# A Mamba-style mixer on TensorE: the z projection of a feature tile issued directly behind its x projection, ahead of the turning of x

## The reference, cut to what matters

```python
proj = input_states @ in_proj_w.T
gate, hBC, dt = jnp.split(proj, [INTER, INTER + CONV_DIM], axis=-1)
x = conv_general_dilated(hBC..., conv_w)              # 4 taps, each feature for itself
hBC = silu(x + conv_b)
hs, Bmat, Cmat = jnp.split(hBC, ...)
xh = hs * dt                                          # and D_res = D * hs
Y_diag = einsum('bclsh,bcshp->bclhp', (C B^T) * exp(segsum(A dt)), xh)
states = einsum('bclhn,bhcl,bclhp->bchpn', Bc, decay_states, xh)   # then carried over chunks
Y_off = einsum('bclhn,bchpn,bhcl->bclhp', Cc, states, exp(A_cum))
y = Y_diag + Y_off + D_res
yg = y * silu(gate)                                   # gate is the "z" of the kernel
out = (norm_w * yg * rsqrt(mean(yg * yg) + EPS)) @ out_proj_w.T
```

## Time and profile before

| what | us |
|---|---|
| median of 3 runs | 2565.89 |
| lowest and highest of them | 2563.54, 2573.93 |
| the profiled execution's own time | 2581.05 |
| its span, first to last instruction | 2579.2 |
| mean granted TensorE clock, share of full | 0.886 |

### The profile page before, as it was taken

The page is one execution under the profiler, slowest core; times in us unless marked ns, Lnnn a source line. Parts: engine busy times, 40 slices in busy tenths (PEclk is TensorE's granted clock), DMA queues, the critical chain, the costliest instruction groups (busy, mean ns, idle before and its releaser), DMA issues.

```text
span 2579.2 us, 45536 instructions
## 1 busy us (share of the span) xinstructions
PE 2068.7 (80%) x12038; PEld 1584.6 (61%) x12043; DVE 1610.5 (62%) x3542; ACT 1416.2 (55%) x3825; POOL 1000.2 (39%) x816
## 2 busy tenths in 40 slices
PE   5896969789459345999999999999999954278883
PEld 4555555455347234888878887888788842156662
DVE  5545555454424476888888888888888863043334
ACT  1443525344224145888878887888788840035542
POOL 0301103030256210444444444444444416737774
PEclk8896978889679676999999999999999976589997
DMA  3451917030446601444434443444344352248878
GB/s 125 159 173 51 290 51 234 1 118 0 181 95 107 166 17 64 137 146 146 147 129 146 146 147 129 146 146 147 130 147 146 114 163 89 103 78 133 133 127 189
DMA packets 193524, 328.61 MB, mean 127 GB/s; under 512 B 19712, under 2 KB 141184, under 8 KB 191104
## 3 DMA queue, kind: packets, MB, share of 16 engines
q1 hardware_dynamic: 162208, 287.54, 35.3%
q0 software_dynamic: 31200, 39.73, 9.8%
HBM read 227.54 MB, written 99.66 MB: 127 GB/s over the span
## 4 chain that ended last, share of the span: by engine, by line
PE 63%; issue 11%; DVE 8%; DMA 4%; POOL 4%; ACT 3%; another core or an unknown queue 3%; PEldq 1%; DVEq 1%; ACTq 1%; SPq 1%; PEld 0%; POOLq 0%
PE bank L1717 14%; PE bank L1771 8%; PE bank L755 6%; PE bank L1745 5%; POOL expert_sums L1107 4%; PE bank L728 4%; PE bank L1764 3%; PE bank L1757 3%; PE bank L744 3%; PE bank L1731 3%; DMA expert_sums<-experts_yo,experts_xt 2%; PE bank L989 2%; PE bank L1740 2%; PE bank L730 2%
## 5 line engine op out<-in xcount | busy, mean ns | idle before, releaser
L1717 PE MATMUL bank<-h_hi,wi 128*128 128x512 f32 x1024 | 404.1, 436 | 0.8 <-ACTq L144 0.8
L1879 DVE SCALAR_TENSOR_TENSOR cv<-bank,cw,cv 128x511 f32<-128x511 f32 (+2 forms) x384 | 287.5, 749 | 84.9 <-ACT cv L1812 51.8
L1107 POOL DMA_INDIRECT expert_sums<-experts_yo,experts_xt x174 | 270.4, 1554 | 144.9 <-ACT experts_yo L1074 117.9
L1806 ACT ACTIVATE l_mat<-l_mat,cum_tok 128x128 f32<-128x128 f32 x1024 | 315.7, 429 | 0.0
L1931 POOL TENSOR_TENSOR xdec<-xdt,dec_tok 128x384 f32<-128x384 f32 x128 | 108.1, 844 | 467.2 <-DVE xdt L1869 467.2
L1946 POOL TENSOR_TENSOR yg<-yd,sgt 128x512 f32<-128x512 f32 x128 | 228.2, 1783 | 76.2 <-DVE yd L1886 76.2
L1198 DVE SCALAR_TENSOR_TENSOR experts_sg<-experts_th,bank 128x96 f32<-128x96 f32 (+2 forms) x190 | 53.9, 284 | 312.8 <-ACT experts_th L1067 187.8
L1771 PE MATMUL bank<-wo,yg 128*128 128x256 f32 x1024 | 242.4, 380 | 0.3 <-POOL yg L1946 0.3
L1717 PEld LDWEIGHTS bank<-h_hi,wi 128*128 128x128 f32 x1024 | 196.1, 191 | 62.7 <-issue 24.2
L579 DVE TENSOR_REDUCE nmax<-bank 128x1 f32<-128x512 f32 (+3 forms) x256 | 114.4, 487 | 177.7 <-PE bank L730 177.7
L657 ACT ACTIVATE work<-bank,nmax 128x512 f32<-128x512 f32 (+3 forms) x256 | 132.8, 525 | 150.1 <-DVE nmax L579 149.9
(11 more groups left out here) (292 smaller groups left out, 4711.0 us busy)
## 6 DMA issues: line engine op xcount, KB each, us to landing
wi<-in_weights_split SPq DMA_DIRECT2D x128, 512.0 KB, 3.5
l_mat<-running_sums SPq DMA_DIRECT2D x128, 512.0 KB, 4.6
experts_xt<-sorted_rows SPq DMA_DIRECT2D x174, 129.0 KB
wo<-out_weights_normed SPq DMA_DIRECT2D x128, 128.0 KB, 2.1
sorted_rows<-blank SPq DMA_DIRECT2D x1, 16383.0 KB, 61.5
expert_sums<-blank SPq DMA_DIRECT2D x6, 2176.0 KB, 17.7
experts_got<-expert_sums SPq DMA_DIRECT2D x24, 512.0 KB, 8.5
w_raw<-in_wi SPq DMA_DIRECT2D x32, 256.0 KB, 3.0
```

Source lines behind the costliest of these rows:

```text
L1107: e.indirect_dma_start(sums[layer][q % SPREAD], bass.IndirectOffsetOnAxis(xt[:, q % LOADED, D + 1:D + 2].bitcast(U32), 0), yo[:, q % YIELD ...
L1717: mm = e.matmul(dst[:, :], l, r[:, k, tok], start=(n == 0), stop=(n == 3 * KD - 1))
L1806: last = e.activation(part, part, ACT.Relu, bias=cum_tok[:, c, hh, bass.ds(w.g, 1)], scale=-1.0)
L1879: e.scalar_tensor_tensor(out=cv[:, w.two, n:SEQ], in0=PSX[w.two][:, 0:SEQ - n], scalar=cw[:, bass.ds(w.f, 1), TAPS - 1 - n], in1=cv[:, w.t ...
```

## The change

On PE, the block that issues the z projection of `tiles[0]` moves up: it now stands directly behind the x projection of the same tile, ahead of T of `tiles[1]` and of the y products of `tiles[3]`. Its wait (`s_sg` of the tile before) and its signal (`s_z`) move with it. No instruction is added or removed, and the lists of DVE, ACT, POOL and SP stay as they are.

```diff
             e.wait_ge(s_wi[w.four], w.loaded_i)
             e.wait_ge(s_tap, done(w.g - 2, 3))
             project(w, PSX[w.two], D, s_x)
+        w = tiles[0]
+        if w.live:
+            e.wait_ge(s_sg, done(w.g - 1))
+            project(w, PSZ, 0, s_z)
         w = tiles[1]
         if w.live:
             e.wait_ge(s_xc, done(w.g))
@@
             mm.then_inc(s_y, 1)
-        w = tiles[0]
-        if w.live:
-            e.wait_ge(s_sg, done(w.g - 1))
-            project(w, PSZ, 0, s_z)
         w = tiles[1]
         if w.live:
             e.wait_ge(s_xdec, done(w.g))
```

## The result

The changed kernel takes 2620.16 us (median of 4 runs, 2614.51 to 2625.42) against 2567.18 of before (4 runs beside it): a ratio of 1.020, 95% interval 1.017 to 1.023, or 44 to 59 us slower. Forecast was 2611, range 2593 to 2631.

A forecast was written before the change was run, and what follows sets the result against it. A ring of ACT and DVE was taken to hold the step at 8.06 us; loop steps +40, fixed-index steps +5.8, four others +2.5, boundaries -2.3, start +1, drain -0.5 gave +46.5, rounded +45: 2611 us, range 2593 to 2631.

The forecast's parts named there:

- The bound before: Loop step before the change: ACT and DVE hold it at 8.06 us; PE alone could do 7.83.
- rival (c): Faster: PE is the bound and z covers its 0.23 wait for `st` in 100 steps; 2541 us, chance 0.05.
- the ring through POOL: T, `xdt`, `xdec`, SS, off-diagonal y, output, x, z, back to T: forecast at 8.46 us a step.
- The chain T, `xdt`, `xdec`, SS: From T over DVE and POOL to SS: 2.52, plus 0.1 for SS behind a wait, 2.62 us; PE idle about 0.6.
- The ring: T to next T in the changed loop: 2.62 + 5.84 = 8.46 us, 0.40 more a step.
- Steps at the turn of the loop: No term in the sum; loop steps expected all alike, 0.95 to `xdec` used only for the range's high end.
- Steps with fixed indices: 12 short steps with fixed indices: 8.31 us each, +0.48 each, +5.8 us in all.
- Boundaries and start: Three group boundaries 0.75 us earlier each, -2.3; second step of the stream waits for `sgt`, +1; drain at the end -0.5.
- The sum: Whole stream: all terms together +46.5 us, rounded to +45, for a median of 2611 us.
- (a): PE's clock falls because of the pauses: 2650 us if every fourth step, 2770 if every step; chance 0.04.
- (b): No measurable difference: T to SS within 2.22 us, step stays 8.06, only boundaries gain; 2564 us, chance 0.06.
- (d): z on PE waits for `sgt` in every step, and T with it; 2636 us at 0.2 beyond the margin, chance 0.02.

The follow-up runs named there:

- before_cv_and_square_between: Kernel before, with `cv` between the two heads' `l_mat` differences on ACT and the square of tile 4 ahead of `cv`: 0.9904 of before, 2541.5 us.
- after_off_before_sums: Changed kernel with the off-diagonal y issued ahead of the state sums on PE: 0.9977 of before.
- before_cv_between: Kernel before, with `cv` issued between the two heads' `l_mat` differences on ACT: 0.9993 of before.
- after_off_before_sums_cv_between: Changed kernel with off-diagonal y ahead of the state sums on PE and `cv` between the heads' differences on ACT: 0.9910 of before.

## Why the prediction was right, point by point

**The bound before.** Right, and shown by before_cv_and_square_between: with PE's list untouched the step falls to 7.82, so PE's 99.5% were not the bound. Busy time hid the pause: a 512-column matmul is shown 0.40 long and the next can begin 0.23 behind it, so of the 0.21 that T waited in the earlier trace rows only 0.04 shows as idle. The same 1321 or 1322 matmuls are 192.44 us busy before and 187.79 there. The forecast of rival (c), that the change would uncover those 0.23, failed where the text said it would: the ring through POOL is longer than both.

**The chain T, `xdt`, `xdec`, SS.** Forecast 2.52 and 0.1 for the start behind a wait. Measured 0.74 + 0.86 + 0.84 + 0.06 = 2.50 in the rows above, and 0.94 for the six products where 0.83 stood. PE's pause was forecast at 0.6 and is 0.55.

**The ring.** Forecast 8.46, measured 8.42 to 8.45 in three of four steps. 0.40 a step was expected and 8.43 - 8.06 = 0.37 came there.

**Steps at the turn of the loop.** This term was left out of the sum, and the text expected steps "all alike". In the trace of before `xdec` starts 0.95 behind `xdt` instead of 0.86 in every fourth step, the first of each turn of the hardware loop, and it was only used as an end of the range. In the changed kernel it is on the ring. In the second group T to `xdt` is also longer in these steps, and by half as much (0.83) in the last two:

```profile
1351.32 0.60 PE L1735 MATMUL bank<-ident,xc 128*128 128x128 f32 x4
...
1352.27 0.69 DVE L1869 TENSOR_TENSOR xdt<-bank,dt_tok 128x512 f32<-128x512 f32 x1 [0.94 <-PE bank L1735]
...
1353.23 0.84 POOL L1931 TENSOR_TENSOR xdec<-xdt,dec_tok 128x384 f32<-128x384 f32 x1 [3.94 <-DVE xdt L1869]
```

0.95 and 0.96 where 0.74 and 0.86 are usual. Such steps take 8.52 in the first group, 8.73 in the second and 8.62 in the last two: 24 of them without those right behind the start or a boundary, some 5 us in all. The average over the 24 steps shown first, all of the first group, is 8.45 with them.

**Steps with fixed indices.** Forecast 8.31, measured 8.23 to 8.25: T to SS is 2.30 there, not 2.37, because DVE follows T by 0.63 to 0.64 instead of the 0.70 of the first tile. There are 9 such intervals, not 12: the interval ahead of each three of them, 7.86 to 7.87 before, became a loop step of 8.43. That moves the sum by less than 1 us.

**Boundaries and start.** Forecast -2.3 for three boundaries; the intervals over them went from 15.44 to 14.46, -2.9. The one behind each varies in both kernels (9.4 to 10.1 in the three profiles of before, 8.7 to 10.7 in those of after), and with it the granted clock there: 9.40 at 0.82 and 9.91 at 0.77 before, 8.70 at 1.00 and 10.74 at 0.71 after. The start was forecast at +1. The first T came 2.1 later, as the bound said, but the four intervals behind it were 3.3 shorter (34.0 to 30.7), and in the two later profiles of before, where they take 31.7, only 1.0. So it is between -1 and +1. The end of the stream, forecast at -0.5, did not change: 15.5 from the last T to the end of the last sum of squares in both.

**The sum.** 46.5 by its terms, +45 as given; 43 to 47 measured in the stream. Part of that agreement is luck: a loop step was forecast 0.03 too long, 2 to 3 us in all, and the turns of the loop, 5 us, were left out. The timed difference of 53 is 8 more than the +45. The interval of the ratio reaches down to 44, and the rest of the program is not the same from one execution to the next; which of the two it is, is open.

**Rivals.** (a), the clock: not seen in the steps of the loop, 1.00 with pauses of 0.55 and of 1.45 a step. The Trainium skill, page "TensorE: Matmul & The Clock Gate", section "A second HAM failure mode: psum-queue depth-cycling", tells of a kernel with short pauses between groups of matmuls whose clock swings; the traces here do not show it at these pauses. (b) needed T to SS within 2.22: it is 2.50. (d), z waiting for `sgt`: in the loop PE has no such wait, only at the start of the stream. In after_off_before_sums, where the step is 8.05, the weight loads of L1717 do show one (76 times between 1100 and 2030 us, 18.4 us in sum, longest 0.3), and PE's matmuls none.

## What to carry to other kernels

An engine that is busy 99% of a loop need not be its bound: look for the steps that take less with the same work, and add up the rings that close over several engines. A piece of work that stands between an engine's request and its use of the answer is cover: it hides the time that the answer takes. Before it is moved, take the round trip from rows in which nobody else was late, and see what is left in between. When a test shortens one ring and nothing comes of it, look at instructions that have become longer, not only at waits.

## What the runs showed of the hardware

A wait is answered quickly here, in the loop of the changed kernel: 0.14 from the end of T on PE to `xdt` on DVE, 0.17 from DVE to POOL, 0.06 from POOL to PE. In the steps with fixed indices the first two are 0.1 shorter (T to `xdt` 0.63 for 0.74, `xdt` to `xdec` 0.77 for 0.86). The first step of each turn of a hardware loop is answered later, by 0.1 on POOL and by up to 0.2 on DVE, with a size that differs from loop to loop (four loops with the same body); what causes it was not tried. And the overlap of POOL and DVE on SBUF operands moved with small shifts of phase: in before_cv_between `xc` starts 0.5 to 1.1 behind the start of a sum of squares that takes 1.28, and is up to 1.35 long; in after_off_before_sums_cv_between it starts mostly 1.46 to 1.52 behind it and is 0.69. With the sum of squares out of the way the kernel went from 0.9993 to 0.9904 of before.
